# Hybrid block on one Trainium2 core: twelve slot buffers, residual products held back, and the output product moved ahead of the value blocks

## What is computed

```python
scores = xf @ router_w + router_b
topk_p, topk_i = jax.lax.top_k(jax.nn.softmax(scores), 2)
h = einsum('td,edh->teh', xf, w1) + b1
gated = silu(einsum('teh,ehf->tef', h, wg) + bg) * (einsum('teh,ehf->tef', h, wv) + bv)
y = einsum('tef,efd->ted', gated, w2) + b2
out = einsum('ted,te->td', y, gates)      # gates: top-2 probabilities, 0 elsewhere
```

## Time and profile before

| | us |
|---|---|
| median of 3 runs | 502.95 |
| lowest, highest | 501.46, 508.21 |
| profiled execution, its own time | 502.02 |
| its span, first to last instruction | 500.1 |

### The profile page before, as it was taken

How to read it: one execution, slowest core, us unless ns; L and a number is a source line. 1 busy time by engine, 2 the same in 40 slices (tenths; PEclk the granted TensorE clock), 3 DMA queues, 4 the chain that set the end, 5 groups by cost and what they waited for, 6 DMA issues and landing times.

```text
span 500.1 us, 10372 instructions
## 1 busy us (share of the span) xinstructions
PE 396.8 (79%) x2676; PEld 291.4 (58%) x2676; DVE 300.5 (60%) x1063; ACT 264.7 (53%) x661; POOL 225.0 (45%) x315
## 2 busy tenths in 40 slices
PE   0899899999999999997787710787878787876867
PEld 0466566756666666655454410677767777666767
DVE  3424657677999999999987654234333334334413
ACT  1236476767888888887645510344434444334503
POOL 6013223135666666666645553045444445445520
PEclk9999999889999999999988755789888989889997
DMA  8525635532444443344400014222221222221159
GB/s 301 185 81 166 185 103 145 141 109 72 118 119 117 117 111 105 93 119 112 114 24 22 29 38 117 55 63 64 65 63 57 62 76 63 65 64 55 54 174 350
DMA packets 43212, 52.20 MB, mean 104 GB/s; under 512 B 8208, under 2 KB 35760, under 8 KB 43024
## 3 DMA queue, kind: packets, MB, share of 16 engines
q1 hardware_dynamic: 38208, 40.97, 28.5%
q0 software_dynamic: 4544, 9.38, 5.9%
q10 hardware_dynamic: 416, 1.33, 0.9%
HBM read 33.70 MB, written 19.76 MB: 107 GB/s over the span
## 4 chain that ended last, share of the span: by engine, by line
PE 41%; DVE 14%; DMA 13%; issue 10%; ACT 10%; SPq 5%; POOL 3%; ACTq 1%; DVEq 1%; POOLq 0%
PE MX L1102 4%; PE EX L1112 4%; PE EX L1316 3%; PE PV L1124 3%; PE W L1268 3%; PE W L1283 3%; ACT prob L584 2%; PE W L1249 2%; DMA kvT<-slots 2%; POOL res L571 2%; DMA res<-ys,oT 2%; DMA res<-ys,kvT 2%; DVE mneg L885 2%; DMA oT<-slots 2%; DVE gT L1055 2%
## 5 line engine op out<-in xcount | busy, mean ns | idle before, releaser
L885 DVE TENSOR_REDUCE mneg<-MX 128x2 f32<-128x512 f32 x128 | 85.3, 684 | 5.3 <-PE MX L1102 3.4
L584 ACT ACTIVATE prob<-EX 128x512 f32<-128x512 f32 x128 | 71.6, 597 | 17.5 <-PE EX L1112 16.4
L510 POOL DMA_INDIRECT slots<-rows,dest x64 | 63.3, 989 | 28.0 <-DVE dest L874 13.8
L1047 DVE COPY Ae<-A 128x512 f32 x39 | 17.7, 455 | 84.3 <-PE PV L1316 47.2
L1102 PE MATMUL MX<-kst,qst 96*128 96x256 bf16 (+1 forms) x256 | 50.7, 281 | 4.7 <-DVE mneg L885 4.3
L1112 PE MATMUL EX<-qst,kst 99*128 99x256 bf16 (+1 forms) x256 | 47.9, 283 | 4.5 <-ACT prob L584 3.3
L571 POOL DMA_INDIRECT res<-ys,kvT x28 | 26.9, 959 | 50.4 <-ACT ys L736 46.1
L1326 PEld LDWEIGHTS W<-w2s,gT 128*128 128x128 f32 x312 | 44.3, 206 | 6.7 <-issue 3.9
L720 ACT COPY xT<-MX 128x256 f32<-128x256 f32 x39 | 14.3, 367 | 62.4 <-PE PV L1316 25.8
L1326 PE MATMUL W<-w2s,gT 128*128 x312 | 44.2, 288 | 3.1 <-DVE gT L1055 1.6
L1316 PE MATMUL EX<-xT,Ae 128*128 128x256 f32 x156 | 44.3, 411 | 0.0
(11 more groups left out here) (177 smaller groups left out, 866.9 us busy)
## 6 DMA issues: line engine op xcount, KB each, us to landing
qk_parts<-parts SPq DMA_DIRECT2D x16, 384.0 KB, 2.8
qst<-qk_parts SPq DMA_DIRECT2D x16, 192.0 KB
kst<-qk_parts SPq DMA_DIRECT2D x16, 192.0 KB
X<-in_x SPq DMA_DIRECT2D x4, 512.0 KB, 7.7
wgv<-in_wg SPq DMA_DIRECT2D x8, 256.0 KB, 3.1
wgv<-in_wv SPq DMA_DIRECT2D x8, 256.0 KB, 3.3
qst<-qk_parts SPq DMA_DIRECT2D x16, 128.0 KB
kst<-qk_parts SPq DMA_DIRECT2D x16, 128.0 KB
```

The costliest lines, as they stand in the source:

```text
L510: pool.indirect_dma_start(out=slots, out_offset=bass.IndirectOffsetOnAxis(ap=dest[q][:, n, k:k + 1], axis=0), in_=rows[q][:, n, k, :], in_ ...
L584: act.activation(prob[:, h, :, :], EX[h % 2][:], ACT.Exp, scale=SCALE).then_inc(s["ex_ok"], 1)
L885: dve.tensor_reduce(mneg[p][:, 2 * pair:2 * pair + 2, k], MX[c % 2][:], AX.X, ALU.max, negate=True).then_inc(s["mx_ok"], 1)
```

## The change

Three edits. The slot buffers become twelve: six new SBUF tensors `xt0` to `xt5` behind the six aliases, six more semaphores, and SP waits for the scatters of tile j - 12 instead of j - 6. On TensorE the value blocks of tile j are issued behind the output product of tile j - 1 instead of ahead of it, with the waits that they had. And ahead of the residual products of bank 3 TensorE waits until all scatters have landed, so that those of banks 3 to 7 come after that.

```diff
-LANES = 6
+LANES = 12
...
         xt = ([pair_of_rows(t, "p k n -> p (k n)") for t in kvT] + [pair_of_rows(t, "p a r -> p (a r)") for t in oT]
-              + [pair_of_rows(t, "p a r -> p (a r)") for t in onrm])
+              + [pair_of_rows(t, "p a r -> p (a r)") for t in onrm]
+              + [sb(f"xt{p}", [P, 2, ROW])[:] for p in range(LANES - 6)])
...
                     need(pe, s["sg_ok"], i - 1, 2)
                     pe.wait_ge(s["Ae_ok"], i + 1)
                     pe.wait_ge(s["xT_ok"], i + 1)
-                    for n in range(4):
-                        if n == 2:
-                            need(pe, s["gT_ok"], i - 1, 2)
-                        o = (gate_b, val_b)[n // 2][q][:, n % 2, :]
+                    for n in range(2):
+                        o = gate_b[q][:, n, :]
                         f = slice(n * P, (n + 1) * P)
                         mm = pe.matmul(o, Ae[q][:, f], xT[q][:], start=True, stop=True)
-                        if n % 2 == 1:
-                            mm.then_inc(s[("gate_mm", "val_mm")[n // 2]], 1)
+                    mm.then_inc(s["gate_mm"], 1)
                 i, q = j - 1, (j - 1) % 2
                 if within(i):
                     e = expert_of(pe, words, i)
...
                     mm.then_inc(s["y_mm"], 1)
+                i, q = j, j % 2
+                if within(i):
+                    need(pe, s["gT_ok"], i - 1, 2)
+                    for n in range(2, 4):
+                        o = val_b[q][:, n % 2, :]
+                        f = slice(n * P, (n + 1) * P)
+                        mm = pe.matmul(o, Ae[q][:, f], xT[q][:], start=True, stop=True)
+                    mm.then_inc(s["val_mm"], 1)
 
             free = ((s["xT_ok"], ST), (s["sg_ok"], 2 * ST), (s["gT_ok"], 2 * ST), (s["yb_ok"], ST))
             for n, bank in enumerate(banks):
                 pe.wait_ge(*free[n // 2])
+                if n == 3:
+                    for lane in range(4):
+                        pe.wait_ge(s[f"res_st{lane}"], 32 * len(range(lane, ST, 4)))
```

More of the change, by code:

```diff
@@ L360, in hybrid_block @@
             row_st0 row_st1 cend_ok cnt_mm cnt_ok tab tab_ok pad_st pad2_st slot_ld0 slot_ld1
-            slot_ld2 slot_ld3 slot_ld4 slot_ld5 xT_mm xT_ok Ae_ok gate_mm val_mm sg_ok gT_ok
+            slot_ld2 slot_ld3 slot_ld4 slot_ld5 slot_ld6 slot_ld7 slot_ld8 slot_ld9 slot_ld10 slot_ld11 xT_mm xT_ok Ae_ok gate_mm val_mm sg_ok gT_ok
             y_mm yb_ok ys_ok b2_ld res_st0 res_st1 res_st2 res_st3 sum fin_mm fin_ok out_st
```

## The result

The changed kernel takes 519.32 us (median of 4 runs, 517.72 to 521.72) against 504.25 us for the kernel before in the same measurement: ratio 1.0297, interval 1.0212 to 1.0381. It is slower. The forecast was 511.8 us in a range of 504 to 520, with 51% for "same" and 45% for "slower". The profiled execution took 519.53 us, its span is 517.6 us, 17.5 more than before. Medians are over all executions of a kernel; ratios and their intervals leave out those more than 1.5% above the kernel's fastest, and the profiles of order_alone and buffers_silu_gt are of such an execution.

A forecast was written before the change was run, and what follows sets the result against it. Slot-load waits and clock falls were taken to bound the expert stretch; the new order's loop gives +10.5 us there, the tail -0.7, so 502.02 plus 9.8 makes 511.8 us. Forecast's own range 504.7 to 514.7, stated range 504 to 520.

The forecast's parts named there:

- The slot waits go, and with them the falls of the clock: Expert stretch: twelve buffers remove TensorE's 27.4 us of slot-load waits and the clock loss, estimated 12 us for seven falls.
- The new order closes a loop through ScalarE and VectorE: Expert tiles: end of value blocks, copy xT, silu, gT, output product y, next value blocks; 4.28 us a tile.
- Its length, 4.28 us: Loop time per expert tile, summed from 1.98, 0.28, 0.99 and 1.03 us; bounds 4.11 and 4.34.
- the 0.28 from gT's end to y: Loop term: wait from the end of VectorE's gT to the start of output product y, taken between 0.21 and 0.34 us.
- The last two tiles, 3.44 us: End of expert stretch: no xT copy, silu no longer waits for the value blocks, so the loop shortens to 3.44 us.
- 1.0 us for a fall of the clock at the pause ahead of y(0): Before the first output product: TensorE idles 2.5 us, and 7/12 x 1.7 us is charged for a clock fall.
- POOL no longer behind, -0.7 us: After the last tile: last scatter starts 3.82 us after y(38) instead of 4.55, giving back 0.7 us.
- The hold-back costs nothing: Kernel's tail: held-back residual products of banks 3 to 7 take 4.7 us and fit in 5.9; cost and gain 0.
- the second rival, rival 2: Expert stretch: the clock swings at the short pauses in every tile, seven falls of 1.7 us, 522.7 us; 14%.
- This part by itself would leave 39 tiles at 2.8 to 2.9 us: Expert stretch: twelve slot buffers without the new order would let each tile take 2.8 to 2.9 us.
- The other loops are shorter: Expert tiles: ScalarE's, VectorE's and POOL's loops stay below the 4.28 us loop; POOL needs 2.5 us a tile.

The follow-up runs named there:

- order_alone: Kernel before with only TensorE's new order, six slot buffers and nothing held back: 526.13 us, ratio 1.0218 to before.
- buffers_silu_gt: Kernel before with twelve slot buffers, TensorE's old order, silu ahead of copy xT and gT ahead of copy Ae: 465.02 us, ratio 0.9153.
- before_again: Kernel before, unchanged, run again beside the changed kernel on the same chip: 511.73 us, ratio 1.0041.
- after_again: Changed kernel, unchanged, run again beside the kernel before on the same chip: 523.04 us, ratio 1.0317 to before.
- silu_first: Changed kernel with ScalarE's silu of tile j ahead of its copy xT of tile j+2: 506.36 us, ratio 0.9866 to before.
- silu_gt_first: Changed kernel with silu ahead of copy xT on ScalarE and gT ahead of copy Ae on VectorE: 491.60 us, ratio 0.9552 to before.
- buffers_alone: Kernel before with twelve slot buffers and nothing else changed: 480.30 us, ratio 0.9439.
- old_order: Changed kernel with the value blocks back ahead of the output product, twelve buffers and hold-back kept: 487.65 us, ratio 0.9485 to before.

## Why the prediction was right, and where it was off

- **The slot waits go, and with them the falls of the clock.** Right: 27.4 us of waits became 1.0, the stage's clock 1.00.
- **The new order closes a loop through ScalarE and VectorE.** Right, and shown by changing its parts: 4.37, 3.85, 3.46 us. This is the mechanism of the prediction, and it holds.
- **Its length, 4.28 us, was short by 0.09; over 36 tiles 3.2 us.** The failed term is the 0.28 from gT's end to y. I had taken the middle of two waits of before, 0.21 at y(0) and 0.34 at y(38). In the changed kernel it is 0.20 at y(0), 0.26 at y(1) and 0.30 to 0.36 in the tiles after. The program makes y(0) wait for one semaphore and y(j) from the third tile on for two; that fits the difference, but no run changed it alone. The upper end of my bounds, 4.34, was the right choice: without three odd tiles the mean is 4.345, and the three (4.59, 4.70 and 4.65, the same in both profiles) add the other 0.9 of the 3.2 us. In the first two gT starts 1.07 and 1.09 us after silu instead of 0.73, in the third silu starts 0.57 instead of 0.30 us after xT. The late gT of the second, tile 14, stands in the kernel before as well (1.08), so it is not the order's; why that tile is late I don't know.
- **The last two tiles, 3.44 us.** Right: 3.47 and 3.46.
- **1.0 us for a fall of the clock at the pause ahead of y(0).** It did not come in the first profile; TensorE paused 2.50 us there. In the second the clock was at its lower level until 325.5, and that is in the 327.5 at which y(0) starts there. order_alone had the fall, behind a pause of 1.86 us.
- **POOL no longer behind, -0.7 us.** Wrong, and so was its ground. The last scatter starts 4.55 us after y(38), as before. POOL was not behind in the kernel before either: it had been idle for 0.40 us when it took up ys(37) at 474.64. In both kernels ys(37) comes only 1.8 us ahead of ys(38) (473.96 and 475.76; 490.94 and 492.75), because yb(37) stands behind gT(38) on VectorE, and POOL needs 2.5 us for a tile's two scatters. I had looked at the tile time and not at the spacing of ys in the last tiles. In before_again the last scatter came 5.17 us after y(38), because y(37)'s signal was held by 2 us; that is most of the -0.8 us behind the stretch in that pair, and has nothing to do with this term.
- **The hold-back costs nothing.** Right, by itself 1.0026.
- **The time.** The sum of the terms gave +9.8 us; the pair of profiles of one chip gives +10.8. The repeated runs rather give more: +15.1 between the medians of the first measurement, and a ratio of 1.0317 in the second, whose interval stands for some 9 to 24 us. The first pair of profiles differs by 17.5 us, 4.2 of them ahead of the stretch, in a part that is alike in both kernels; how much of the medians' difference lies there no profile shows. y(38) came at 490.86 and not near 484, for this 4.2 us and 2.3 more in the stretch. I had left the spread of that part out of the range's working. The forecast's own range, 504.7 to 514.7, misses the measured 519.32. The stated range holds it by 0.7 us only because it was widened for the second rival, which did not come: luck. The likelier verdict of the prediction, "same", did not come either.
- **What rival 2 stood for, a clock that swings at short pauses,** did not come: 38 pauses of 0.6 to 2.5 us, clock 1.00 in all of them, and 1.00 again in after_again, silu_first and silu_gt_first. (Its price stands as 522.6 in one place and 522.7 in another; the sum is 522.7.) The rule of the Trainium skill ("TensorE: Matmul & The Clock Gate", section "A second HAM failure mode: psum-queue depth-cycling") is not borne out by this case, with products in float32 and TensorE busy 116.4 of 164.25 us.
- **"This part by itself would leave 39 tiles at 2.8 to 2.9 us"** was wrong for the buffers alone: 3.2. I had taken three flowing tiles for a rate that lasts. "The other loops are shorter" is true against 4.28 us and false against 2.83: the loop of yb, ys, xT, silu and gT is 2.88 us long, and the held signals come on top of it.

## What to carry to other kernels

When products are moved on TensorE, write down what every other engine's queue waits for at the end of the moved group, and add up the loop that comes back to TensorE; here the same order of TensorE costs 1.53, 1.01 or 0.62 us a tile over the flowing 2.84, by what stands ahead of what on ScalarE and VectorE. Work whose input has long been ready (silu) does not belong behind a copy that waits for a later event; with twelve buffers and the old order the exchange of two blocks on each of two engines took the stretch from 122.1 to 110.5 us. More buffers help only as far as the wait that they remove is not followed by another in the same gap.

Then add up the loops that leave the moved engine out. Once TensorE flows, the loop between ScalarE and VectorE sets the tile. A consumer that falls further behind its producer from tile to tile, at the same step each time, shows such a loop: look first at what stands ahead of the consumer in its own queue, and only then at the producer.

## What the runs showed of the hardware

TensorE kept up a tile's products at 2.84 us for thirteen tiles without a pause, at a granted clock of 1.00, and raised each semaphore 0.29 or 0.39 us after the start of the last pass (buffers_silu_gt).

In buffers_alone and old_order, again and again, and once at the end of before_again, TensorE's semaphores go up late and several at once: in the place shown of buffers_alone, four groups whose last passes start from 387.54 to 389.38 are announced between 390.29 and 390.45. Recorded starts of products are then no measure of when the others can go on. The cause was not found.

The part ahead of the expert stretch, the same instructions in all kernels, took between 312.65 and 327.07 us in twelve profiles. Half-clock stretches in it come at different places and in different numbers. They are the likeliest cause, but this was not tested.
